# An fp32 feed-forward kernel: GpSimd's elementwise operations in pieces of 256 columns, and another order of VectorE's work where one block of tokens follows another

## The reference

```python
xn = _layernorm(x, axis=-1)
# branch A: half of each token's 2752 gated values, those of smallest magnitude, are set to zero
s = silu(einsum('bsh,ih->bsi', xn, w_gate))
_, idx = top_k(-abs(s), k)          # k = 1376
flat = s.reshape(B * S, I).at[rows, idx].set(0.0)
s = flat * einsum('bsh,ih->bsi', xn, w_up)
s = einsum('bsi,hi->bsh', s, w_down)
# branch B
g = silu((silu(xn @ W_gate.T) * (xn @ W_up.T)) @ W_down.T)
x = x + s * g
```

## Time and profile before

| | |
|---|---|
| median of 3 runs | 2782.82 us (2781.74 to 2786.43) |
| the profiled execution | 2784.59 us, span 2782.8 us |
| PE busy | 2753.9 us, 99% of the span |
| DVE busy | 2307.4 us, 83% |
| ACT busy | 1352.7 us, 49% |
| POOL busy | 388.3 us, 14% |

### The profile page before, as it was taken

One profiled execution on the slowest core, in us unless ns is written; L12 is line 12 of the kernel. 1 busy time (PEld: TensorE's weight loads), 2 busy tenths in 40 slices (PEclk: granted clock), 3 DMA queues, 4 the chain that ended last, 5 costly groups with the idle time before them and its releaser, 6 DMA issues. The chain is left out here.

```text
span 2782.8 us, 31374 instructions
## 1 busy us (share of the span) xinstructions
PE 2753.9 (99%) x12204; PEld 2281.1 (82%) x12204; DVE 2307.4 (83%) x3002; ACT 1352.7 (49%) x1386; POOL 388.3 (14%) x161
## 2 busy tenths in 40 slices
PE   9999999999999999999999999999999999999999
PEld 7778888878788888888878888888887888888887
DVE  7676999999967698998986678999897767999971
ACT  4234998332444477631144557671115446776110
POOL 5565443044400000000020000000011000000000
PEclk9999999999999999999999999999999999999999
DMA  6898888579766555556656655555666664555564
GB/s 235 308 328 286 293 288 280 211 251 357 255 193 196 181 188 192 189 203 219 249 190 195 192 180 190 195 196 194 240 223 195 193 196 173 195 196 193 189 233 170
DMA packets 135097, 614.28 MB, mean 221 GB/s; under 512 B 12752, under 2 KB 12752, under 8 KB 89168
## 3 DMA queue, kind: packets, MB, share of 16 engines
q1 hardware_dynamic: 134992, 612.94, 63.2%
HBM read 492.31 MB, written 120.59 MB: 220 GB/s over the span
## 5 line engine op out<-in xcount | busy, mean ns | idle before, releaser
L632 PE MATMUL ps<-w_split,hid_ring 128*128 128x512 f32 x4096 | 935.2, 390 | 6.8 <-ACT hid_buf L1136 4.6
L632 PEld LDWEIGHTS ps<-w_split,hid_ring 128*128 128x128 f32 x4096 | 769.4, 188 | 171.5 <-issue 7.9
L1380 DVE TENSOR_SCALAR_CACHE_REDUCE ranks<-key_buf,cand 128x2752 int16<-128x2752 f32 x248 | 762.9, 3076 | 5.8
L961 ACT ACTIVATE signs_row<-key_buf,cand 128x2752 bf16<-128x2752 f32 x248 | 642.6, 2591 | 191.6 <-DVE cand L1389 182.0
L877 PE MATMUL ps<-xnT,w_split 128*128 128x512 f32 x1376 | 535.3, 389 | 0.0
L876 PE MATMUL ps<-xnT,w_split 128*128 128x512 f32 x1376 | 535.3, 389 | 0.0
L875 PE MATMUL ps<-xnT,w_split 128*128 128x512 f32 x1376 | 535.3, 389 | 0.0
L1206 POOL TENSOR_TENSOR w_split<-w_raw,w_split 128x1024 fp32r<-128x1024 f32 (+2 forms) x118 | 290.2, 2467 | 377.3 <-ACT w_split L928 137.0
L875 PEld LDWEIGHTS ps<-xnT,w_split 128*128 128x128 f32 x1376 | 258.3, 188 | 53.7
L876 PEld LDWEIGHTS ps<-xnT,w_split 128*128 128x128 f32 x1376 | 258.3, 188 | 53.6
L877 PEld LDWEIGHTS ps<-xnT,w_split 128*128 128x128 f32 x1376 | 258.3, 188 | 53.3
(11 more groups left out here) (146 smaller groups left out, 2907.0 us busy)
## 6 DMA issues: line engine op xcount, KB each, us to landing
w_split<-split SPq DMA_DIRECT2D x272, 1024.0 KB, 4.8
split<-w_split SPq DMA_DIRECT2D x72, 1024.0 KB, 6.8
w_raw<-w_a SPq DMA_DIRECT2D x100, 512.0 KB, 4.2
w_raw<-t_dram SPq DMA_DIRECT2D x78, 512.0 KB, 3.3
w_raw<-w_b SPq DMA_DIRECT2D x42, 512.0 KB, 4.9
w_extra_raw<-t_dram SPq DMA_DIRECT2D x42, 512.0 KB, 3.6
t_dram<-t_buf SPq DMA_DIRECT2D x20, 1024.0 KB, 8.6
w_extra_raw<-w_a SPq DMA_DIRECT2D x30, 512.0 KB, 3.6
```

The lines of the kernel that those rows point to most:

```text
L632: ins = pe.matmul(ps[:, 2 * t + half, :], h, w[:, half * TB:(half + 1) * TB], start=(first and n == 0), stop=last and stop)
L961: act.activation(signs_row[:, :], keys[:, t, :], ACT.Sign, bias=cand_f[:, t:t + 1], scale=-1.0, accum_out=counts[:, t:t + 1]).then_inc(act ...
L1380: dve.tensor_scalar(ranks[:, :], keys[:, t, :], cand_f[:, t:t + 1], 0.0, ALU.is_lt, ALU.add, accum_out=counts[:, t:t + 1]).then_inc(sel_st ...
```

## The change

Each of GpSimd's elementwise operations is issued as pieces of 256 columns, and only the last piece signals: an operation of 1024 columns becomes four instructions, one of 768 three, one of 512 two. The four sums of x are cut likewise into four. Nothing about which operation follows which changes on GpSimd.

On VectorE two things move at each of the three block changes: the low part of the next block's weight tile 2 goes from ahead of the first gating product to behind it, and the low parts 6 and 7 of x go from the beginning of the new block to ahead of the fourth gating product. On TensorE, ScalarE and SP nothing changes.

```diff
+PIECE = 256
+
+
+def pieces(w):
+    return [slice(c, c + PIECE) for c in range(0, w, PIECE)]
...
-                pool.tensor_tensor(w_lo[q][:, 0:w], w_raw[q][:, 0:w], w_hi[q][:, 0:w].bitcast(F32),
-                                   ALU.subtract).then_inc(lo_ready, 1)
+                for cols in pieces(w):
+                    ins = pool.tensor_tensor(w_lo[q][:, cols], w_raw[q][:, cols], w_hi[q][:, cols].bitcast(F32), ALU.subtract)
+                ins.then_inc(lo_ready, 1)
...
-                pool.tensor_tensor(stage[:, 1, :], w_stage_raw[s % STAGES][:, :], stage[:, 0, :].bitcast(F32),
-                                   ALU.subtract).then_inc(stage_lo, 1)
+                for cols in pieces(H):
+                    ins = pool.tensor_tensor(stage[:, 1, cols], w_stage_raw[s % STAGES][:, cols], stage[:, 0, cols].bitcast(F32),
+                                             ALU.subtract)
+                ins.then_inc(stage_lo, 1)
...
+            def s_chunks(out, in0, in1, op):
+
+                for k in range(4):
+                    ins = pool.tensor_tensor(out[:, k, :], in0[:, k, :], in1[:, k, :], op)
+                ins.then_inc(s_raw, 1)
...
-                    pool.tensor_tensor(x_res[:, t, :], x_res[:, t, :], silu_g[:, t, :], ALU.add).then_inc(out_ready, 1)
+                    for cols in pieces(H):
+                        ins = pool.tensor_tensor(x_res[:, t, cols], x_res[:, t, cols], silu_g[:, t, cols], ALU.add)
+                    ins.then_inc(out_ready, 1)
...
                 if b > 0:
-                    for n in (6, 7):
-                        xn_low(b, n)
                     last_outputs(b - 1, OUT_POOL)
...
-                    w_lows(b + 1, 0, 3)
+                    w_lows(b + 1, 0, 2)
                 for t in range(NT - 1 if last_block else NT):
+                    if not last_block and t == 1:
+                        w_lows(b + 1, 2, 3)
+                    if not last_block and t == NT - 1:
+                        for n in (6, 7):
+                            xn_low(b + 1, n)
```

More of the change, by code:

```diff
@@ L1226, in s_sum @@
                 if n == 0:
-                    pool.tensor_tensor(s_row(1), s_feat(0, tok2), s_feat(1, tok2), ALU.add).then_inc(s_raw, 1)
+                    s_chunks(s_row(1), s_feat(0, tok2), s_feat(1, tok2), ALU.add)
                 elif n == 1:
                     pool.wait_ge(s_raw, (b - 1) * 4 + 1)
-                    pool.tensor_tensor(s_row(0), s_row(1), s_feat(0, tok1), ALU.subtract).then_inc(s_raw, 1)
+                    s_chunks(s_row(0), s_row(1), s_feat(0, tok1), ALU.subtract)
                 elif n == 2:
-                    pool.tensor_tensor(s_row(2), s_feat(0, tok1), s_feat(0, tok2), ALU.subtract).then_inc(s_raw, 1)
+                    s_chunks(s_row(2), s_feat(0, tok1), s_feat(0, tok2), ALU.subtract)
                 else:
                     pool.wait_ge(s_raw, (b - 1) * 4 + 3)
-                    pool.tensor_tensor(s_row(3), s_feat(1, tok1), s_row(0), ALU.subtract).then_inc(s_raw, 1)
+                    s_chunks(s_row(3), s_feat(1, tok1), s_row(0), ALU.subtract)
             for m in range(TILES):
```

## The result

The changed kernel took 2821.5 us (median of 4 runs, 2818.9 to 2822.6), the kernel before 2782.8 us: ratio 1.0139, 95% interval 1.0127 to 1.0151. It is 38.7 us slower. Slower was forecast, but by 16.4 us.

The account below looks back on a forecast made before the run. PE was busy 99%, so only TensorE's waits and clock could matter. Two block changes 10.8, slabs 2, masks through first change 3.6: 16.4 us on 2782.8 gave 2799 us, range 2776 to 2811.

Parts of the forecast that it names:

- the chain of the third addition: Second and third block change: GpSimd's late third addition delays tile 7's load and P5; 5.4 us for each change.
- the slabs: Block 0's slabs: low parts in pieces let VectorE's turns in and end later; about +2 us, bounds -4 and +12.
- Alternation, one instruction each: Shared SBUF ports: with work queued on both, VectorE and GpSimd take turns; pieces 0.7 us alone, 1.1 to 1.8 beside VectorE.
- The rival in which the hand-over favours the next piece: Block changes: third addition isn't starved, additions end at about 1426, P5 starts at 1434.4; 2772 us, chance 0.22.
- third addition ends 13.35 us behind: Second and third change: four pieces alternate with four VectorE operations, so the third addition ends at 1430.4, today 1424.1.
- P5 10.2 us behind the third addition: Block changes: store, tile 7's load, high parts and low parts follow the third addition before P5 starts, at 1440.6.
- The half clock, 2.4 forecast: Block changes: TensorE's clock at half behind the long wait before P5, costing 2.4 us.
- The masks, -3.1: Block 0's masks: VectorE waits for pieces, not whole operations; gains 2 us there, 1.1 at the next stage's beginning.
- The stretch up to the first change: From eight GpSimd operations to P5: +3.7 for pieces, -2.4 gating product, +3.0 third addition's chain, plus 2.4 half clock.
- eight operations: Ahead of the first change: eight GpSimd operations as 32 pieces take 26.3 us instead of 22.6, +3.7.
- The wait for `xnT`, 2.06 to 0.9: Second and third change: TensorE's wait for low part 6 of x falls from 2.06 to about 0.9 us.
- block 0 gets worse: Block 0's slabs: late staged low parts hold SP's loads up in every third tile, +12 us; 2810 us, chance 0.13.

Follow-up runs that it names:

- e10: The changed kernel with pieces of 512 columns instead of 256 in the low parts and additions; 2799.2 us.
- e3: The kernel before with pieces only in GpSimd's low parts of block 0's slab tiles and of the staged tiles, old VectorE order; 2795.8 us.
- e4: The kernel before with pieces only in the three additions of outputs at each block change, old VectorE order; 2802.8 us.
- e6: The kernel before with pieces only in GpSimd's low parts computed while VectorE makes block 0's masks; 2778.4 us.
- e2: The kernel before with all of GpSimd's operations in pieces of 256 columns, VectorE's order unchanged; 2819.5 us.
- e5: The changed kernel with its three additions of outputs at each block change whole again; 2798.8 us.
- e9: The changed kernel with SP's stores of the third and fourth output put behind the load of weight tile 8; 2808.3 us.
- e7: The kernel before, no pieces, VectorE's low part 6 of x moved behind the second gating product and 7 behind the third; 2783.9 us.
- e8: e7 plus pieces of 256 columns in GpSimd's low parts during block 0's masks only; 2782.4 us.
- e11: e8 with SP's stores of the third and fourth output put behind the load of weight tile 8; 2773.8 us.
- e15: The kernel before with only SP's stores of the third and fourth output put behind the load of weight tile 8; 2779.5 us.

## Why the prediction was right in direction and wrong in size

The forecast was 2799 us, its range 2776 to 2811, and 2821.5 us were measured. The direction and the chain of the third addition held; two terms of the sum were too small, the slabs' most of all.

- **Alternation, one instruction each: right.** Pieces last 0.7 us alone, and the twelve of a change 15.14 us, 1.26 each. Turns, not the fixed part, make up the loss (e10). The rival in which the hand-over favours the next piece is out: the additions end 14.65 us behind the old block's end, not below 10.
- **The slabs, "about +2; bounds -4 and +12": the step that failed.** It measured 13.4 us with those pieces alone (e3) and 14.2 in the changed kernel's trace, beyond the bounds, which the prediction itself named as a sign of being wrong. The prediction costed one low part at 1.7 us with a half clock and added 2 for all others, and took the lateness of a staged low part only as the upper bound. Both halves cost by themselves (8.7 and 5.4), since low part, spill, load and high part form a loop in which lateness is handed on.
- **The chain of the third addition, +5.4 us each: right mechanism, undersized.** e4 gives 20.4 us for three changes, 6.8 each; in the changed kernel P5 to P5 it is 7.4 and 8.0. The term "third addition ends 13.35 us behind" measured 14.65: already the last piece of the second addition met an operation of 1024 columns (1.80 us at 1444.56), a fifth turn where the prediction counted four. "P5 10.2 us behind the third addition" measured 11.8: tile 7's high part starts 5.1 us behind the issue, not 4.1, with a store and four more loads issued within some 4 us behind it, and the steps from there to P5 take 6.25 us, not 5.6. The half clock, 2.4 forecast, measured 2.5 at the second change.
- **The masks, -3.1: right as far as can be told.** 3.6 us alone (e6), with an interval of 0.8 to 6.4. In the changed kernel TensorE makes up 3.6 us there (15.5 to 11.9). But e2, whose code is the same up to there, still waits 4.13 us for `hid_buf` in its trace and makes up 0.4, and e5 and e9 make up 2.4 each.
- **The stretch up to the first change** (+3.7 for eight operations, -2.4, +3.0): TensorE loses 8.0 us from the end of the masks to P5, where 4.3 were forecast. The waits for the eight operations' low parts grow by 3.8 us, from 1.22 at 714.69 to 3.89 and 1.12 at 727.00 and 747.39, which is the +3.7; the half clock behind the 3.89 wait (0.50 from 725.81 to 732.64) was left out, and so was the one behind the masks' wait, 2.4 us, which is gone (1.00 from 624.92 to 629.00). The gating product's 2.4 us go, as forecast. P5's wait grows from 0.58 to 8.27 us, the same chain as at the other changes. The stretch of eight operations wasn't tried alone.
- **The wait for `xnT`, 2.06 to 0.9: right** (1.00), but a gain that another wait takes back: the order alone gave nothing. Nor is the order needed for it: with the old order the pieces in the additions alone bring this wait to 0.86 us (e4, second and third change), since low part 6 then waits for one piece and not for a whole addition.
- **What is left**: e2 less e3 and e4 is 3.3 us, and with the masks' gain some 7 us of pieces in the other stages. These weren't separated.

The rival "block 0 gets worse" (2810 us, 0.13) named the right place with almost the right price (+12), but beside an undersized chain: 12 in place of 2 and 8 in place of 5.4 thrice gives 10 + 8 more, 2817 us, which is within 5 us of the measured time. The 8 is the measured figure, so this names the terms that were too small and isn't a forecast.

## What to carry to other kernels

Where two engines take turns at a port, cutting one engine's operations gives the other a turn at each cut: it pays where the other is late and little waits for the cut one (the masks, 3.6 us, uncertain in size), and costs where the cut one releases something, most of all in a loop of low part, store, load and high part, where one price is paid on every lap. Before a wait is shortened, look at what is second-latest at the same place: here the reordering showed no gain while SP's stores stood ahead of the loads (e7, e8), and moving them gave 8.6 us there (e8 to e11), against 3.0 us, not clear of nothing, without it (e15). Put a queue's loads that somebody will need ahead of stores that wait for a late engine.

## What the runs showed of the hardware

- The same wait doesn't always cost clock. In the kernel before, TensorE starts again at 1421.99 behind 2.06 us and is at half from 1423.40. With the two stores later (e15) it starts again behind 2.05 us at the same matmul, and the stretch behind it (us, busy times, PEclk, DMA share, GB/s) has full clock:

```profile
1421.33 3.00 PE L848 MATMUL ps<-w_extra,xnT 128*128 128x512 f32 x12 [2.05 <-DVE xnT L1346]
```

```profile
1421.33:1429.61 8.28, 8.28 (x36) 6.84 (x37) 8.28 (x7) 4.43 (x5) 2.12 (x1) 1.00 0.71 226
```

Nor is it the stores: in e3, whose stores and order are those of before, the second change has the half clock behind this wait and the third hasn't, at matmuls of the same place.

```profile
1433.15 4.58 PE L859 MATMUL ps<-w_extra,xnT 128*128 128x512 f32 x12 [2.07 <-DVE xnT L1366]
...
2113.92 2.99 PE L859 MATMUL ps<-w_extra,xnT 128*128 128x512 f32 x12 [2.06 <-DVE xnT L1366]
```

```profile
1434.30:1437.20 2.90, 2.90 (x9) 2.22 (x8) 2.90 (x3) 0.37 (x2) 0.95 (x1) 0.50 1.01 352
2115.00:2118.00 3.00, 3.00 (x15) 2.48 (x14) 3.00 (x3) 0.46 (x2) 1.03 (x1) 1.00 0.99 359
```

What differs ahead of it wasn't found; so the 1.7 us of a half clock behind a short wait can't be counted on as a gain.
- The same load takes longer where more is issued around it: tile 7's high part starts 4.1 us behind the issue in the kernel before, where one store follows at once, 5.1 us in the changed one, where a store stands right ahead of it and a store and four loads follow within some 4 us, and 5.7 us in e7 (1423.26 to 1429.00), with a store on either side. With the stores moved behind, in e15, it is 3.1 us (1424.37 to 1427.45). How much each neighbour adds wasn't separated.
- The shared port holds for a whole instruction in both directions down to pieces of 0.7 us: VectorE's 1024 columns beside them are recorded with 1.76 us (1445.68) in place of 1.2, and a piece beside them with 1.80 (1444.56) in place of 0.7. The Trainium skill (SBUF — State Buffer, "Who interferes with whom") says that the shared pair is an exclusive lock and that the order of issue decides which of the two is blocked; the trace agrees, and shows besides that with both queues full the turns alternate strictly.
